# Softmax sums ahead of the sums of squares, values' product sooner, GpSimd's roots ahead of the scaled values

## What is computed

```
xm = expmap0(layer_norm(logmap0(x)) * (1 + sc_msa) + sh_msa)
q, k, v = to_heads(plin(xm, w_q, b_q)), ... k, ... v        # plin: expmap0(logmap0(x) @ w + b)
scores = einsum(qt, kt) / sqrt(16); attn = softmax(scores)
out_h = expmap0(einsum(attn, vt))
attn_t = g_msa * logmap0(plin(from_heads(out_h), w_o, b_o))
x = mobius_add(residual, expmap0(attn_t))
...                                                         # then the same again with a two-layer MLP
return x_in + block(x_in)
```

## Time and profile before

| | us |
|---|---|
| median of 3 runs | 765.44 |
| lowest, highest | 763.75, 766.3 |
| the profiled execution, its time | 765.7 |
| the profiled execution, its span | 763.9 |

### The profile page before, as it was taken

How to read it: one execution, slowest core, us unless ns; L and a number is a source line. 1 busy time by engine, 2 the same in 40 slices (tenths; PEclk the granted TensorE clock), 3 DMA queues, 4 the chain that set the end, 5 groups by cost and what they waited for, 6 DMA issues and landing times. The chain is left out here.

```text
span 763.9 us, 27111 instructions
## 1 busy us (share of the span) xinstructions
PE 644.4 (84%) x8419; PEld 464.3 (61%) x8433; DVE 654.1 (86%) x2171; ACT 524.7 (69%) x1563; POOL 347.0 (45%) x683
## 2 busy tenths in 40 slices
PE   4956889999999999999999997605669999999996
PEld 2645667777777777777777775402326566656664
DVE  2786788999999999999999997485998999999975
ACT  1123567777777777777777775334879989999874
POOL 1003556666666666666666665111234244234321
PEclk9978899999999999999999998656999999999999
DMA  9942876666666666666666665222444455445523
GB/s 321 359 116 57 141 131 137 146 141 143 141 147 142 145 142 147 141 141 144 147 140 147 144 133 113 50 70 70 124 124 133 139 158 163 149 132 166 164 72 110
DMA packets 184804, 107.50 MB, mean 141 GB/s; under 512 B 140188, under 2 KB 167591, under 8 KB 184744
## 3 DMA queue, kind: packets, MB, share of 16 engines
q1 hardware_dynamic: 182952, 103.99, 55.6%
q10 hardware_dynamic: 1792, 2.89, 1.0%
HBM read 64.11 MB, written 9.18 MB: 96 GB/s over the span
## 5 line engine op out<-in xcount | busy, mean ns | idle before, releaser
L885 PE MATMUL p_qkv<-wqkv,tT 128*128 128x256 f32 x768 | 198.1, 396 | 5.5 <-DVE u L1143 5.5
L885 PEld LDWEIGHTS p_qkv<-wqkv,tT 128*128 128x128 f32 x768 | 139.7, 195 | 22.9 <-issue 6.3
L899 PEld LDWEIGHTS p_o<-v,pT 64*64 64x64 f32 x4096 | 66.7, 136 | 21.9 <-issue 21.9
L899 PE MATMUL p_o<-v,pT 64*64 64x17 f32 x4096 | 73.0, 210 | 0.0
L858 PE MATMUL p_oz<-wo,oT 128*128 128x256 f32 x256 | 69.7, 397 | 0.0
L445 POOL TENSOR_TENSOR rt<-ss_t,c_mhalf 128x1 f32<-128x1 f32 x64 | 42.1, 658 | 60.6 <-ACT junk L634 53.7
L659 ACT ACTIVATE pT<-p_s 128x1024 f32<-128x1024 f32 x64 | 65.6, 1024 | 2.8 <-PE p_s L875 1.7
L1143 DVE SCALAR_TENSOR_TENSOR u<-p_qkv,ct,bqkv 128x768 f32<-128x768 f32 x64 | 64.3, 1005 | 3.5 <-PE p_qkv L885 3.5
L617 ACT ACTIVATE oT<-p_oz 128x256 f32<-128x256 f32 x64 | 24.6, 384 | 57.0 <-PE p_oz L850 57.0
L504 POOL TENSOR_TENSOR rt<-ss,c_mhalf 128x2 f32<-128x2 f32 x32 | 26.5, 827 | 80.8 <-ACT wqkv L707 80.8
L933 PE MATMUL p_t<-ident,pT 128*128 128x128 f32 x128 | 21.3, 290 | 46.5 <-ACT pT L714 46.5
(11 more groups left out here) (275 smaller groups left out, 1685.2 us busy)
## 6 DMA issues: line engine op xcount, KB each, us to landing
mod<-mod_rows SPq DMA_DIRECT2D x128, 128.0 KB, 2.9
x_all<-in_x SPq DMA_DIRECT2D x8, 1024.0 KB, 14.3
gate<-mod_rows SPq DMA_DIRECT2D x128, 64.0 KB, 2.7
mod<-mod_rows SPq DMA_DIRECT2D x32, 256.0 KB, 4.2
mod_b<-mod_rows SPq DMA_DIRECT2D x32, 256.0 KB, 4.4
out<-x_all SPq DMA_DIRECT2D x32, 256.0 KB, 3.0
gate<-gate_rows SPq DMA_DIRECT2D x32, 128.0 KB, 2.9
bqkv<-gate_rows SPq DMA_DIRECT2D x32, 128.0 KB, 2.9
```

Of the source, the lines that this page charges most:

```text
L885: mm = pe.matmul(p_qkv[:, a * D:a * D + D], tT[:, k, c, :], wqkv[:, c, a * D:a * D + D], start=c == 0, stop=c == C - 1)
L899: mm = pe.matmul(p_o[S * e:S * e + S, col:col + VW], pT[keys, e, g, :], v[keys, k, 2 * g + e, :], start=True, stop=True, skip_group_check= ...
```

## The change

Three engines get another order within a slot; no instruction is added or taken away, and all waits keep their counts. On VectorE `softmax_sums`, `clip_t` and `normalise` go ahead of `sum_squares` and `sum_rows`. On TensorE `attend` goes ahead of the k part of `qkv`, where it was ahead of the v part. On GpSimd `head_roots` goes ahead of `scale_v`.

```diff
@@ slot of GpSimd
                 if on(h, off, L_E):
                     low_parts(2 * h + off - L_E, (off - L_E) % 2, h + (off - L_E) // 2)
-                    scale_v(2 * h + off - L_E, (off - L_E) % 2)
                 if on(h, off, L_D):
                     head_roots(2 * h + off - L_D)
+                if on(h, off, L_E):
+                    scale_v(2 * h + off - L_E, (off - L_E) % 2)
                 if on(h, off, L_G):
                     keep_stats(2 * h + off - L_G, (off - L_G) % 2)
@@ slot of TensorE
                     qkv(i, k, 0)
-                    qkv(i, k, 1)
                 if on(h, off, L_L):
                     attend(2 * h + off - L_L, (off - L_L) % 2)
                 if on(h, off, L_C):
+                    qkv(i, k, 1)
                     qkv(i, k, 2).then_inc(qkv_psum, 1)
@@ slot of VectorE
-                if on(h, off, L_D):
-                    sum_squares(2 * h + off - L_D)
-                    sum_rows(2 * h + off - L_D)
                 if on(h, off, L_L):
                     softmax_sums(2 * h + off - L_L)
                 if on(h, off, L_C):
                     clip_t(2 * h + off - L_C, (off - L_C) % 2)
                 if on(h, off, L_L):
                     normalise(2 * h + off - L_L)
+                if on(h, off, L_D):
+                    sum_squares(2 * h + off - L_D)
+                    sum_rows(2 * h + off - L_D)
                 if on(h, off, L_E):
                     repeat_parts(2 * h + off - L_E, (off - L_E) % 2, h + (off - L_E) // 2)
```

## The result

The changed kernel takes **909.87 us** (median of 4 runs, 906.71 to 911.43) against 765.25 us before; the ratio is 1.190, with a 95% interval from 1.187 to 1.193. The forecast was 896 us, in a range from 874 to 927. The profiled execution took 909.23 us, with a span of 907.4 us, 143.5 us longer than before.

What follows compares the result with a forecast made beforehand. The loop through `o`, 6.26 us a slot, was taken as the bound; the change makes `u` wait for `v`, 8.57 us with clock. Over 53 slots, with 3 us lateness, +118.8, plus 12 at the ends, +130.8: 896 us, range 874 to 927.

Steps and rivals of the forecast that it cites:

- The bound before: Attention half: the loop from `g_all` through `o`, its transpose and the output product sets the slot, 6.26 us.
- VectorE's own 6.18 us: Next limit once the loop through `o` is shortened: VectorE's 5.34 us from `u` to `u` plus 0.84 us of copies.
- The wait at `u`: `u` waits for GpSimd's `v`, now behind `head_roots`: 3.13 us from second `hs`, 5.34 back, slot 8.47 us against 6.26.
- `roots` at 0.29 us: GpSimd's `roots` takes the first tile's 0.29 us, not mid-kernel's 0.40, as VectorE stands still; with 0.40 the slot is 8.58.
- TensorE's clock: Idle about 2 us a slot slows the four rows ahead of `attend`: 0.10 us a slot taken, 0.30 for the range.
- The sign of 70% busy for both engines: Sign that the forecast is right: VectorE and TensorE both near 70% busy in mid-kernel.
- The ends: Some ten slots filling or draining, each taking between nothing and 2.2 us more: 12 us taken of 22.
- The sum: 53 slots x 8.57 = 454.2 us plus 3 of lateness, +118.8 us; with 12 at the ends +130.8, so 896 us.
- the lateness: 6.6 us over the 53 slots before; 3 kept for 0.23 us gaps every fourth slot, late loads dropped.
- the bound at half clock: Rival: gaps hold TensorE at 1.2 GHz, its work at most 9.6 us a slot, 55 us more, 951 us; chance 0.07.
- VectorE's own work as the bound: Rival, faster: no wait at `u` and a shorter chain at `rlim` and `fac`, slot 6.18 us, 758 us; chance 0.03.
- the second rival: Wait at `u` met early by a miscounted tile; loop closes at `fac`, 6.32 us a slot, 766 us; chance 0.02.

Runs made afterwards that it cites:

- The fourth kernel: VectorE's and TensorE's parts of the change, without GpSimd's, against the kernel before: 761.4 us, ratio 0.996.

## Why the prediction was right, point by point

- *The bound before* was the loop through `o`. The fourth kernel shows that it was not the only one: taking 1.10 us out of it left the slot at 6.26 us. I had written that this loop falls to 5.16 us and that VectorE's own 6.18 us comes next. The first left out TensorE's v product, which stands ahead of the transpose of `o` and lets it come only 0.33 us sooner; the second left out the way through the roots, which is as long as the old loop. Both were incomplete, without a price here.
- *The wait at `u`* was right, in place, in kind and in size. Forecast: 3.13 us from the second `hs` to `u`, 5.34 back, 8.47 in all. Measured: 388.87 to 392.13 is 3.26 us, a slot without disturbance 8.46. Inside, two terms were off and cancelled, so the agreement to 0.01 us is luck. From the end of `v` to `u` it is 0.23 us (391.90 to 392.13), where I had taken 0.09 from the copy behind `low_parts`. And VectorE's way back is 5.20 us in an undisturbed slot (5.38 in the one shown, with the 0.19 us ahead of `o`), for I had counted `junk` and `o` at their full length, while the next instruction starts 0.08 us before their end. In GpSimd's part alone, where `o` is not in the way, they cancel less: 3.33 us to `u` and 4.58 back, 7.91 against my 7.77. The idle ahead of `u` is 2.79 us and not the 2.3 that I gave as a sign, since the copies in front of it shrank to 0.29 us each.
- *`roots` at 0.29 us* was right, and so the choice of the first tile's row over mid-kernel's.
- *TensorE's clock* is the term that was mis-sized. I took 0.10 us a slot and 0.30 as its upper bound. The mean slot is 0.39 us above the undisturbed one, 20.5 us in all; filling the gap brought back 18.4 of them, 0.35 us a slot. The other 2 us are the every-fourth slots, for which I had kept 3. The bound of 0.30 failed because I let only the four rows ahead of `attend` slow down, and took `attend` at its 1.12 us. At 1.2 GHz it takes 1.91 us, so both together can be 1.7 us late, not 0.6. In the low-clock stretch that I had looked at, `attend` came when the clock was back. The sign of 70% busy for both engines was off for the same reason on TensorE, 82% between 200 and 300 us; VectorE was at 64%.
- *The ends* were right: I took 12 us, and the slots outside the 53 grew by 13 us.
- *The sum*: 53 slots at 8.85 us are 468.9 us where I had 457.2. The clock is 13.1 us above my 5.3, the lateness and the undisturbed slot 1.4 below what I took. With 1 us more at the ends this is all of the 12.7 us between the forecast and the profiled execution. The range held although the clock had passed its bound, because its high end also had room for `roots` at 0.40 us, all of the lateness and 22 us at the ends.
- *The rivals.* TensorE did not become the bound at half clock; it was busy 82% between 200 and 300 us, at a mean granted clock of 0.84 and not 0.50. The wait at `u` was not met early. VectorE's own work as the bound is what a third buffer would have to reach for, and it does not: with it the slot is 6.54 us, not 6.18, and VectorE idles 0.49 us of it ahead of `g_all`. The loop that closes at `fac`, the second rival, I had priced at 6.32 us, 3.13 to `fac` and 3.19 back. There it took 3.44 and 3.10: `fac` did not wait for `v` itself, it started 0.34 us behind the end of `v`, because `rlim` had been held up by `v` and `lnx` stood behind it.

## What to carry to other kernels

Before moving an instruction behind another in an engine's queue, list what waits for the moved one, for each buffer that it frees as much as for each value that it makes: here a wait for a free buffer, harmless for as long as `v` ran early, put ScalarE and GpSimd in series with VectorE. Such a wait does not show in a profile of the kernel before; it has to be read from the program, with the tile that it counts. And when a loop is shortened, close all other loops through the same engines on paper first: two of them may be within a tenth of a microsecond of the one that is seen.

## What the runs showed of the hardware that was not expected

- With a gap of 2 us in most slots of 8.5 us TensorE spent part of the time at 1.2 GHz (mean granted clock 0.84 between 200 and 300 us), and three products a slot on data that nobody uses brought it to 1.00 and made the kernel 19 us faster. In GpSimd's part alone, with waits for `u` of at most 1.4 us in that stretch, it was 1.00 as well.
- `attend`, 64 rows of 17 columns, takes 1.12 us at the one clock and up to 1.91 us at the other: these small products lose nearly as much as the four rows of `p_qkv`, 1.13 and 2.00 us.
- A VectorE instruction of 3 columns with two inputs in SBUF took 0.56 us instead of 0.16 beside GpSimd's `v`; a step of GpSimd on 51 columns took 0.45 us instead of 0.27 when it started 0.10 us behind VectorE's `junk`, and 0.33 us when it started 0.25 us behind it.
